# QR sign recursion of a rotation stage: Gram pivots and sign pivots of the same 32 columns in one loop, beside moved weight and constant work

## The chip, the cores and the metric

One core of a Trainium2 chip runs the whole program. Its engines work in parallel and meet at semaphores: TensorE (PE, with its weight loads as PEld), VectorE (DVE), ScalarE (ACT), GpSimd (POOL) and SyncE (SP), which issues the DMAs. The metric is the device time in microseconds of one execution.

## The reference, cut to what matters

Inputs are x (8 x 128 x 144) and a condition vector of 144 numbers for each of the 8 batch elements. Layer 0 rotates x inside the column space of a matrix P (144 x 64); three transformer layers with adaptive scale and shift, 16-head attention and a GELU MLP follow (24 visits of one batch element and layer).

```
def _rotation(cond, W, b):
    v = silu(cond) @ W.T + b                 # 2016 numbers for each batch element
    A = skew-symmetric 64 x 64 matrix from v
    return expm(A)                           # R, 64 x 64
# layer 0:  Q, _ = qr(P);  x = x + (x Q)(R - I) Q^T      (as the kernels compute it)
```

R comes from a polynomial and seven squarings. Q is not computed: with the Gram matrix G = P^T P and its Cholesky-like elimination, x Q follows from x P and the inverse factor. What remains of a Householder QR is the sign of each column, and those 64 signs come from a recursion over the top 64 x 64 part of P, one pivot after another.

## The kernel before

Everything here lies in one function, `program`, with one instruction list for each engine; the order in which the code is written is the order in which an engine executes. No scheduler changes it.

**The pivot work on DVE.** All of it is on 32-partition tiles, with three loops one after the other. Each `need(...)` waits for DVE's own counter, so an instruction that reads what the one before wrote waits for its completion.

- First loop (L1262 to L1301): 31 elimination steps of the leading 32 columns of G, in `lead`, with the inverse beside them. A step is four instructions: `spread` (a stream shuffle that copies row j to all 32 partitions, L1259), a reciprocal, a factor, an update of 64 columns. Some other work is put into steps 4, 6 and 24 (constants; the unpacking of the skew matrices, `LEAD_TAKES`).
- Second loop (L1320 to L1343): 32 steps on `work`, which holds the sign recursion of the leading half (columns 0 to 63) and the elimination of the trailing half of G (columns 64 on) side by side. A step is a 129-column spread, the sign fix of the pivot (L1326), a reciprocal of two numbers, two factors (L1330, L1332) and two updates (L1336, L1339).
- Third loop (L1368 to L1383): 31 steps of the sign recursion of the trailing half in `last`, five instructions each.

Between the loops, small products on TensorE (`lead_products`, `work_products`) form the Schur complement and turn factors; GpSimd takes one square root for each half (`root`, L405).

**What the other engines do meanwhile.** TensorE and ScalarE work through the list `pre` (`plan_rotation`): upper, skew, n2, mods, n4, gate 0, poly (1,0), gate 1, poly (1,1), gate 2, poly (0,0), xp, poly (0,1), two expm steps and the squarings. `lead_products` stands in TensorE's list behind n2 and `work_products` behind the squaring (4,1); each holds what is behind it until DVE's loop has ended. The last skew power, `raw`, the transposed `zT` (product of `linvT` and `xpT`) and DVE's scaling of `raw` by the signs (`rmi`, L1396) meet in the product that gives `yT`; from there it is a fixed path to the first visit.

**Weight remainders.** The last 17 rows of four weight matrices are used as three bf16 parts. For each layer ScalarE casts a part and makes a masked copy (`weight_part`, L575 and L577, into space of `gmod`), GpSimd subtracts it (`weight_left`, L411, 12 pieces of 102 x 268), and this is done twice.

**Constants.** GpSimd makes the scaled identities `eyes`, `irep` and `identb`, and TensorE's list waits for the last of them.

Of the kernel before, what the change touches and what calls it, by code (L numbers as in the profile page):

```python
# [26 lines left out]
BF16 = mybir.dt.bfloat16  # L27
# [7 lines left out]
D = 64  # L35
# [16 lines left out]
WSPLIT = NTAIL // 4  # L52
# [34 lines left out]
LEAD_TAKES = 24  # L87
FIRST_HALF_AFTER = ("n2", 0)
SECOND_HALF_AFTER = ("square", (4, 1))
# [7 lines left out]
def program(nc, t, out, spread_mods):  # L97
    ctx = ExitStack()
    with ctx:
# [41 lines left out]
        pick = sb("pick", [HALF, 2, HALF])  # L141
        nhalf_i = sb("nhalf_i", [HALF, D])
# [6 lines left out]
        lead = sb("lead", [HALF, 2 * D])  # L149
        work = sb("work", [HALF, D + 3 * HALF])  # L150
        ptop = sb("ptop", [HALF, D])
        g11 = sb("g11", [HALF, D])
        arow, brow, crow = sb("arow", [HALF, 2, 2 * D]), sb("brow", [HALF, 2, D + 3 * HALF]), sb("crow", [HALF, 2, HALF])
        arec, brec, crec = sb("arec", [HALF, HALF]), sb("brec", [HALF, HALF, 2]), sb("crec", [HALF, HALF])
        fac = sb("fac", [HALF, 2, 2])
        picked = sb("picked", [HALF, 2, HALF])
        dq, dr = sb("dq", [HALF, 1]), sb("dr", [HALF, 2])
        rs = sb("rs", [HALF, 2])
        scaled = sb("scaled", [HALF, D])
        m0T = sb("m0T", [HALF, HALF])  # L160
        wl = sb("wl", [HALF, HALF])
        zz = sb("zz", [D, HALF])
        last = sb("last", [HALF, HALF])
        sgn = sb("sgn", [HALF, 2])
# [13 lines left out]
        def halves(k):  # L178
# [16 lines left out]
        tprod = gmod[0:KS, 1:3, :, :].rearrange("p l b g -> p (l b g)")[:, 0:LAYERS * NTAIL].rearrange(  # L195
            "p (l n) -> p l n", l=LAYERS)
# [41 lines left out]
        ld = {n: sem("ld_" + n) for n in ("cond", "p", "skw", "x", "misc", "ada0", "ada1", "ada2",  # L238
                                          "blk0", "blk1", "blk2", "tail0", "tail1", "tail2", "tmask", "gmod0", "gmod1", "gmod2")}
        loads = {"cond": 3, "p": 4, "skw": 3, "x": 3, "misc": 3, "ada0": 3, "ada1": 2, "ada2": 2,  # L240
# [9 lines left out]
        lead_done, lead_turned, scaled_ready, m0T_ready = sem("lead_done"), sem("lead_turned"), sem("scaled_ready"), sem("m0T_ready")  # L250
        schur_full, top_full = sem("schur_full"), sem("top_full")
        dq_ready, rs_ready = sem("dq_ready"), sem("rs_ready")
        work_done, wl_ready, linv_turned = sem("work_done"), sem("wl_ready"), sem("linv_turned")
        wp_full, zz_ready, last_full, last_ready = sem("wp_full"), sem("zz_ready"), sem("last_full"), sem("last_ready")
# [6 lines left out]
        tail_cast, tail_left, tailw_ready = sem("tail_cast"), sem("tail_left"), sem("tailw_ready")  # L261
        act_step = sem("act_step")
# [38 lines left out]
        def _(sp):  # L301
# [8 lines left out]
            load(ptop[:], t["ptop"], "p")  # L310
            load(pT2[:], t["pT2"], "p")
# [4 lines left out]
            for l in range(LAYERS):  # L316
                load(tails[:, l, :], t[f"tail{l}"], f"tail{l}")
            for l in range(LAYERS):
# [21 lines left out]
            for l in range(LAYERS):  # L340
                if l == 1:
                    sp.wait_ge(tail_left, 2 * LAYERS)
# [22 lines left out]
        def _(pool):  # L365
# [16 lines left out]
            filled(lead[:, D:2 * D], 1.0).then_inc(early_consts, 1)  # L382
            pool.wait_ge(early_consts, 1)
            step(g.memset(half[:], 0.5))
            step(filled(work[:, D + 2 * HALF:D + 3 * HALF], 1.0))
            step(filled(ident[:], 1.0))
            step(g.memset(notj[:], -1.0))
            step(g.tensor_tensor(notj[:], notj[:], ident[0:HALF, 0:HALF], ALU.add))
# [1363 lines left out]
```

## Time and profile before

| | us |
|---|---|
| three runs | 436.83, 434.18, 437.65 |
| their median | 436.83 |
| the profiled execution | 434.67 |
| its span from first to last instruction | 432.8 |
| first pivot shuffle on DVE | 6.87 |
| second loop begins / third loop begins | 41.76 / 102.37 |
| product of `rmi` and `zT` begins | 137.38 |

The profile is of one execution; its rows give the time from the start of the span, the duration, engine, line, operation, output<-inputs and shapes. Line numbers are those of the kernel before. A duration is from start to completion, so two neighbours on one engine may overlap; the distance of their starts tells how soon the second could go. "PEclk 0.50" is the lower of TensorE's two clock levels (1.2 GHz), 1.00 the higher (2.4 GHz).

### The profile page before, as it was taken

What the parts mean: (1) busy time and instruction counts of PE and PEld (TensorE: products, weight loads), DVE (VectorE), ACT (ScalarE), POOL (GpSimd) and SP (SyncE); (2) the same over time, 40 slices, a digit from 0 to 9 for tenths busy, and PEclk for the clock granted to TensorE, in tenths of its full rate; (3) what the DMA queues carried; (4) which work ended last, traced back from release to release, by engine and by line L of the source; (5) the groups of instructions that cost most, each with busy time, mean ns of one, the idle gap of its engine ahead of it and who ended that gap; (6) DMA issues with size and microseconds to landing.
All of it is one profiled execution on the core that took longest, in us unless ns stands there. A gap on an engine that the chain in (4) does not pass through costs nothing.

```text
span 432.8 us, 10670 instructions
## 1 busy us (share of the span) xinstructions
PE 309.1 (71%) x3653; PEld 223.9 (52%) x3653; DVE 319.5 (74%) x1311; ACT 235.0 (54%) x494; POOL 154.2 (36%) x507
## 2 busy tenths in 40 slices
PE   1705987006003468889999999999999989898746
PEld 0704636005002234657777777777666666667534
DVE  4888999888886464877777877777989898877120
ACT  1420156002301225679787887978787878686721
POOL 7102508001600321253435353444555545442140
PEclk9999998556655555999999999999999999999978
DMA  5685000760000000000000000000000000000000
GB/s 167 198 251 172 0 0 5 195 207 1 0 1 0 2 0 2 2 2 2 5 2 2 2 3 3 2 2 3 2 2 2 3 2 2 2 16 2 15 15 14
DMA packets 10092, 14.10 MB, mean 33 GB/s; under 512 B 1674, under 2 KB 8558, under 8 KB 9912
## 3 DMA queue, kind: packets, MB, share of 16 engines
q1 hardware_dynamic: 10040, 13.43, 10.6%
q8 instruction: 30, 0.49, 0.5%
q14 instruction: 22, 0.18, 0.1%
HBM read 12.80 MB, written 0.62 MB: 31 GB/s over the span
## 4 chain that ended last, share of the span: by engine, by line
DVE 35%; PE 26%; issue 19%; POOL 10%; ACT 8%; SPq 1%; DMA 0%; POOLq 0%; ACTq 0%; DVEq 0%
PE ps L823 18%; DVE nmax L1498 5%; PE ps L1067 4%; DVE brow L1326 3%; DVE brow L1259 2%; ACT skw_r L707 2%; DVE lead L1275 2%; DVE fac L1330 2%; DVE work L1336 2%; PE ps L1124 2%; DVE arow L1259 2%; DVE work L1339 2%; ACT brief L668 2%; DVE fac L1272 2%; ACT L699 1%
## 5 line engine op out<-in xcount | busy, mean ns | idle before, releaser
L1498 DVE TENSOR_REDUCE nmax<-ps 128x4 f32<-128x512 f32 x96 | 62.6, 684 | 30.1 <-PE ps L823 30.0
L682 ACT ACTIVATE skw_t<-ps 128x512 f32<-128x512 f32 x96 | 53.4, 595 | 21.6 <-PE ps L823 21.4
L823 PE MATMUL ps<-skw_r 54*128 54x128 bf16 x768 | 48.4, 224 | 6.0 <-DVE nmax L1498 4.0
L823 PEld LDWEIGHTS ps<-skw_r 54*128 54x128 bf16 x768 | 30.1, 97 | 27.6 <-issue 18.9
L508 POOL TENSOR_TENSOR rstd<-vare,nhalf 128x1 f32<-128x1 f32 x24 | 13.2, 551 | 85.2 <-DVE vare L1416 68.5
L823 PE MATMUL ps<-mT_t,fc1w_t 128*128 128x256 f32 x120 | 39.8, 424 | 1.4 <-ACT mT_t L720 1.3
L823 PE MATMUL ps<-fc2w,skw_r 128*128 128x144 f32 (+1 forms) x240 | 34.2, 290 | 0.6 <-ACT skw_r L707 0.6
L675 ACT ACTIVATE skw_r<-ps 128x512 bf16<-128x512 bf16 x48 | 26.0, 594 | 12.5 <-PE ps L1067 12.1
L823 PEld LDWEIGHTS ps<-fc2w,skw_r 128*128 128x128 f32 (+1 forms) x240 | 30.8, 190 | 2.4 <-ACT skw_r L707 1.3
L1067 PE MATMUL ps<-identb,brief 128*128 128x128 bf16 x384 | 26.9, 226 | 4.9 <-DVE brief L1485 4.7
L699 ACT ACT_TABLE_LOAD x23 | 29.5, 1283 | 0.4
L823 PE MATMUL ps<-nmT,sel 64*128 64x128 bf16 x384 | 28.6, 222 | 0.0
L1067 PEld LDWEIGHTS ps<-identb,brief 128*128 128x128 bf16 x384 | 24.0, 102 | 7.1 <-issue 6.7
L823 PE MATMUL ps<-qkvw_t,hT_t 128*128 128x432 f32 x48 | 25.3, 612 | 0.8 <-ACT hT_u L728 0.8
L823 PEld LDWEIGHTS ps<-mT_t,fc1w_t 128*128 128x128 f32 x120 | 19.2, 201 | 8.9 <-issue 5.0
L494 POOL TENSOR_TENSOR tail<-ln,gmod 128x16 f32<-128x16 f32 x48 | 11.0, 229 | 35.1 <-DVE ln L1429 28.3
L823 PE MATMUL ps<-skw_t,brief 128*32 128x128 f32 x512 | 22.0, 288 | 1.1 <-ACT skw_t L682 1.1
L823 PE MATMUL ps<-skw_t,skw_r 64*64 64x128 f32 x16 | 2.0, 422 | 28.9 <-DVE skw_r L1396 28.9
L411 POOL TENSOR_TENSOR tails<-tails,gmod 102x268 f32<-102x268 f32 x24 | 17.1, 744 | 14.3 <-ACT gmod L577 14.3
L689 ACT ACTIVATE skw_t<-ps 128x512 f32<-128x512 f32 x24 | 14.0, 584 | 11.5 <-PE ps L823 11.1
L707 ACT ACTIVATE skw_r<-ps 128x512 f32<-128x512 f32 (+1 forms) x36 | 18.3, 509 | 3.5 <-PE ps L823 3.5
L668 ACT ACTIVATE brief<-ps 128x432 bf16<-128x432 f32 x32 | 17.7, 561 | 3.3 <-PE ps L823 3.3
(262 smaller groups left out, 813.6 us busy)
## 6 DMA issues: line engine op xcount, KB each, us to landing
gmod<-spread_mods SPq DMA_DIRECT2D x3, 1408.0 KB, 12.7
adaw_t<-in_ada SPq DMA_DIRECT2D x3, 432.0 KB
tails<-in_tail SPq DMA_DIRECT2D x3, 427.1 KB
skw_t<-in_skw SPq DMA_DIRECT2D x1, 1024.0 KB
fc1w_t<-in_fc SPq DMA_DIRECT2D x3, 320.0 KB
fc2w<-in_fc SPq DMA_DIRECT2D x3, 288.0 KB
qkvw_t<-in_qkv SPq DMA_DIRECT2D x3, 216.0 KB
x<-in_x SPq DMA_DIRECT2D x1, 576.0 KB, 6.3
```

Of the source, the lines that this page charges most:

```text
L411: i = g.tensor_tensor(w, w, tprod[:, l, c * WSPLIT:(c + 1) * WSPLIT], ALU.add)
L508: g.tensor_tensor(rstd[:, 0, h:h + 1], vare[:, 0, h:h + 1], nhalf[:, 0:1], ALU.pow).then_inc(rstd1, 1)
L668: a.activation(dst, src, ACT.Copy).then_inc(first_parts, 1)
L675: a.activation(qkT[1][v % 2][:, n:n + 4, :].rearrange("p k t -> p (k t)"), ps[:, 7, :].bitcast(BF16)[:, n * T:(n + 4) * T], ACT.Copy).then ...
L682: a.activation(prob[g].rearrange("p i t -> p (i t)"), ps[:, 2 + g % 2, :], ACT.Exp, scale=SCALE).then_inc(prob_ready, 1)
L689: a.activation(o_raw[v % 2].rearrange("p g t -> p (g t)"), ps[:, 4, :], ACT.Copy).then_inc(o_raw_ready, 1)
L699: a.activation(table_out[:], half[:], f).then_inc(table_used, 1)
L707: a.activation(hid[0:rows, 2 * r:2 * r + n, :, :].rearrange("p c h t -> p (c h t)"), ps[0:rows, FC1_BANKS[r], 0:n * 2 * T], f).then_inc(hi ...
L823: return pe.matmul(o, lhsT, rhs, start=start, stop=stop, skip_group_check=True)
L1067: i = pe.transpose(o[:, pair * T:(pair + 1) * T], parts[k][v % 2][:, 2 * pair:2 * pair + 2, :].rearrange("p h d -> p (h d)"), identb[:])
L1259: return did(d.stream_shuffle(out_, rows, [j] * HALF))
L1498: d.tensor_reduce(nmax[:, v % 2, first:first + 7:2], ps[:, 6 + g % 2, :].rearrange("p (i t) -> p i t", i=4), AX_X, ALU.max, negate=True).t ...
```

## The change

1. The signs are found another way. Per column the new kernel uses beta = sqrt(pivot of G) with the sign of the top entry, den = entry + beta, and updates the top rows with a numerator that uses the elimination factor `gfac` of the same column. So step j of the sign recursion needs step j of the elimination in the same half, and a square root for each column. These 64 roots are single-column powers on GpSimd (`root_of`), which read the pivot that the shuffle has written to a ring of four rows, `grow`.
2. There are two loops on DVE in place of three. In the first, sign step j of the leading half (`top[0]`, 64 columns shrinking to 33) and elimination step j+2 of the leading half alternate; in the second the same for the trailing half (`top[1]`, 32 columns shrinking to 1) with elimination step j+1.
3. Between them three block products on TensorE (`z_product` behind gate 0, `schur_products` behind poly (1,0), `turn_product` behind poly (1,1)) give the trailing Gram matrix and the trailing top part.
4. The product with `linvT` and its copy come at the end of the second loop (after elimination step 30 and sign step 30).
5. Weight remainders: TensorE computes tails - high - middle in PSUM by an identity product in fp32 and masked bf16 identity products (`left`, `rest`), in seven pieces of 512 columns behind "upper"; ScalarE casts each piece twice (`mid_part`, `low_part`). GpSimd's 24 subtractions and ScalarE's masked copies go.
6. ScalarE makes `eyes`, `irep` and `identb`. GpSimd's other small tasks are dealt out between its 64 roots; at roots 3, 46, 52 and 57 they carry waits for a load or for ScalarE. SP loads the top part of P in three pieces; the Gram product waits for two loads in place of four.

On DVE, in the steady part of the pivot work, a step of the second loop stood thus before (names as in the list above; f32 32-partition tiles):

```order
L1259 STREAM_SHUFFLE brow<-work 32x129 [waits dve_step]
L1326 SCALAR_TENSOR_TENSOR brow<-brow 32x1 [waits dve_step]
L1328 RECIPROCAL brec<-brow 32x2 [waits dve_step]
L1330 SCALAR_TENSOR_TENSOR fac<-work,brec,below 32x1 [waits dve_step]
L1332 SCALAR_TENSOR_TENSOR fac<-work,brec,notj 32x1
L1336 SCALAR_TENSOR_TENSOR work<-brow,fac,work 32x64 [waits dve_step]
L1339 SCALAR_TENSOR_TENSOR work<-brow,fac,work 32x55 [waits dve_step]
```

And thus a step of the changed kernel's first loop (trow, beta, den, tnum, drec, tfac, top are the sign recursion; grow, grec, gfac, lead the elimination):

```order
L1337 STREAM_SHUFFLE trow<-top 32x59 [waits dve_step]
L1371 SCALAR_TENSOR_TENSOR beta<-trow,root 32x1 [waits root_ready,dve_step]
L1359 SCALAR_TENSOR_TENSOR lead<-grow,gfac,lead 32x64 [waits dve_step]
L1377 TENSOR_SCALAR den<-trow,beta 32x1 [waits dve_step]
L1378 SCALAR_TENSOR_TENSOR tnum<-gfac,beta,top 32x1
L1381 RECIPROCAL drec<-den 32x1 [waits dve_step]
L1337 STREAM_SHUFFLE grow<-lead 32x65 [waits root_ready,dve_step]
L1385 SCALAR_TENSOR_TENSOR tfac<-tnum,drec,notj 32x1 [waits dve_step]
L1349 RECIPROCAL grec<-grow 32x1 [waits grow_ready]
L1392 SCALAR_TENSOR_TENSOR top<-trow,tfac,top 32x58 [waits dve_step]
L1353 SCALAR_TENSOR_TENSOR gfac<-lead,grec,below 32x1 [waits dve_step]
```

Seven instructions became eleven; between two that depend on each other there is now mostly one of the other recursion.

On TensorE, around the joint of the two loops, the changed list has the three block products between items of `pre`:

```order
L864 MATMUL ps<-kz,lead 32x32 [waits kz_ready,tailw_ready]
L864 MATMUL ps<-irep,eyes 128x256 [waits pre_read]
L864 MATMUL ps<-brief,eyes 128x256
L864 MATMUL ps<-base,zt 32x128 [waits z_ready,ld_base]
L864 MATMUL ps<-zt,base 32x32
L864 MATMUL ps<-adaw_t,s_t 8x352 [waits pre_read,ld_ada1]
L864 MATMUL ps<-adaw_u,s_bd 8x352
L864 MATMUL ps<-irep,eyes 128x256 [waits pre_read]
L864 MATMUL ps<-brief,eyes 128x256
L864 MATMUL ps<-vv,x1T 32x32 [waits vv_ready,x1T_ready]
```

DVE waits for the results of the products with `kz`, `zt` and `vv`; poly (1,0) stands before the second, gate 1 and poly (1,1) before the third.

The diff, cut to its core:

```diff
@@ GpSimd
+            def root_of(i):
+                p, j = i // HALF, i % HALF
+                pool.wait_ge(grow_ready, i + 1)
+                g.tensor_tensor(root[:, p, j:j + 1], grow[:, i % 4, 0:1], half[:], ALU.pow).then_inc(root_ready, 1)
...
-            root(0)
-            for l in range(LAYERS):
-                for c in range(4):
-                    weight_left(0, l, c)
...
+            for i in range(D):
+                root_of(i)
+                if i == 2:
+                    left_masks()
...
+                if 42 <= i < 42 + LAYERS:
+                    tail_mods(i - 42)
+                if i == 46:
+                    pool.wait_ge(pre_read, was_read("mods", 0))
+                if 46 <= i < 52:
+                    turned_mods((i - 46) // 2, i % 2)
...
+                if i == 57:
+                    pool.wait_ge(pre_read, pre_reads[-1])
...
@@ TensorE, behind "upper"
+            def left(c):
+                pe.wait_ge(high_ready, layers_of(c))
+                if c >= 3:
+                    pe.wait_ge(tailw_ready, c - 2)
+                at = chunk(c)
+                o = ps[0:KS, LEFT_BANKS[c % 3], 0:at.stop - at.start]
+                mm(o, ident[0:KS, 0:KS], tails_flat[:, at], True, False)
+                mm(o, dmask[:, 0, :], tailw_flat[:, at], False, False).then_inc(left_full, 1)
+            def rest(c):
+                pe.wait_ge(mid_ready, c + 1)
...
@@ VectorE, first loop of the changed kernel
+            for j in range(HALF):
+                e = j + 2
+                k_row = top_pivot(0, j)
+                k_beta = top_root(0, j, k_row)
+                if e < HALF - 1:
+                    gram_update(0, e, k_fac)
...
+                if j == HALF - 1:
+                    dve.wait_ge(schur_full, 1)
+                    loaded(dve, "base")
+                    k_late = did(d.tensor_tensor(late[:, 0:2 * D], base[1][:], ps[0:HALF, 7, 0:2 * D], ALU.subtract))
+                k_drec = top_denominator(0, j, k_beta)
+                if e < HALF - 1:
+                    gram_pivot(0, e + 1)
...
+                k_tfac = top_factor(0, j, k_drec)
+                if e < HALF - 1:
+                    k_rec = gram_reciprocal(0, e + 1)
...
+                top_update(0, j, k_tfac)
+                if e < HALF - 2:
+                    k_fac = gram_factor(0, e + 1, k_rec)
+                early_extras(j)
...
+            dve.wait_ge(top1_full, 1)
+            upd["t", 1] = did(d.tensor_tensor(top[1][:], late[:, HALF:D], ps[0:HALF, 6, 2 * D:2 * D + HALF], ALU.subtract))
```

## Rows read from the trace of the kernel before

**Rows 1.** Windows by stage: busy us (instructions) of each engine, granted clock, DMA share, GB/s.
```profile
0.00:41.80 41.80, 14.10 (x90) 12.22 (x90) 31.20 (x185) 9.75 (x13) 10.68 (x37) 1.00 0.69 203
41.80:100.20 58.40, 29.37 (x275) 19.06 (x275) 53.70 (x253) 14.56 (x30) 18.26 (x31) 0.78 0.27 76
100.20:136.90 36.70, 7.37 (x102) 5.66 (x102) 30.16 (x205) 7.15 (x10) 8.15 (x40) 0.59 0.00 0
136.90:173.40 36.50, 24.79 (x199) 15.64 (x200) 17.45 (x53) 12.27 (x30) 7.44 (x28) 0.50 0.00 1
```
**Rows 2.** Timeline, start of the pivot work: start us, us, engine, line, operation, shapes.
```profile
5.48 0.22 DVE L1251 TENSOR_TENSOR s_bd<-s_bd,own 119x56 f32<-119x56 f32 x1
...
6.61 0.21 DVE L1256 COPY lead<-ps 32x64 f32<-32x64 f32 x1 [0.92 <-PE ps L823]
```
**Rows 3.** DVE's timeline, two successive shuffles of the first loop.
```profile
30.60 0.21 DVE L1259 STREAM_SHUFFLE arow<-lead 32x65 f32<-32x65 f32 x1
...
31.59 0.21 DVE L1259 STREAM_SHUFFLE arow<-lead 32x65 f32<-32x65 f32 x1
```
**Rows 4.** DVE's timeline, one step of the second loop and the next shuffle.
```profile
50.67 0.28 DVE L1259 STREAM_SHUFFLE brow<-work 32x129 f32<-32x129 f32 x1
...
51.36 0.21 DVE L1330 SCALAR_TENSOR_TENSOR fac<-work,brec,below 32x1 f32<-32x1 f32 x1
51.49 0.20 DVE L1332 SCALAR_TENSOR_TENSOR fac<-work,brec,notj 32x1 f32<-32x1 f32 x1
51.62 0.27 DVE L1336 SCALAR_TENSOR_TENSOR work<-brow,fac,work 32x64 f32<-32x64 f32 x1
51.82 0.27 DVE L1339 SCALAR_TENSOR_TENSOR work<-brow,fac,work 32x62 f32<-32x62 f32 x1
...
52.12 0.28 DVE L1259 STREAM_SHUFFLE brow<-work 32x129 f32<-32x129 f32 x1
```
**Rows 5.** DVE's timeline, the third loop, from one sign fix on.
```profile
103.67 0.15 DVE L1374 SCALAR_TENSOR_TENSOR crow<-crow 32x1 f32<-32x1 f32 x1
103.86 0.15 DVE L1376 RECIPROCAL crec<-crow 32x1 f32<-32x1 f32 x1
104.04 0.21 DVE L1380 SCALAR_TENSOR_TENSOR fac<-last,crec,below 32x1 f32<-32x1 f32 x1
104.28 0.24 DVE L1382 SCALAR_TENSOR_TENSOR last<-crow,fac,last 32x30 f32<-32x30 f32 x1
```
**Rows 6.** Timeline, GpSimd's subtractions beside two instructions of DVE.
```profile
41.14 8.52 POOL L411 TENSOR_TENSOR tails<-tails,gmod 102x268 f32<-102x268 f32 x12
...
42.08 7.59 DVE L1326 SCALAR_TENSOR_TENSOR brow<-brow 32x1 f32<-32x1 f32 x1
...
68.91 0.78 DVE L1332 SCALAR_TENSOR_TENSOR fac<-work,brec,notj 32x1 f32<-32x1 f32 x1
```
**Rows 7.** Timeline, GpSimd's second root and DVE beside it.
```profile
100.78 0.57 POOL L405 TENSOR_TENSOR rs<-dr,half 32x1 f32<-32x1 f32 x1 [26.08 <-DVE dr L1350]
100.91 0.14 DVE L1353 TENSOR_SCALAR sgn<-dr 32x1 f32<-32x1 f32 x1
100.97 0.22 DVE L1355 COPY linvT<-ps 128x64 f32<-128x64 f32 x1
...
101.10 0.30 DVE L1358 SCALAR_TENSOR_TENSOR s<-sgn,rs 32x1 f32<-32x1 f32 x2
```
**Rows 8.** Timeline of TensorE and ScalarE: gates, zT, the first product behind the signs, a cast.
```profile
48.51 1.34 PE L823 MATMUL ps<-adaw_t,s_t 128*8 128x352 f32 x2
...
55.91 0.76 PE L823 MATMUL ps<-adaw_t,s_t 128*8 128x352 f32 x2
...
61.09 0.60 ACT L613 ACTIVATE skw_t<-ps 128x512 f32<-128x512 f32 x1 [1.63 <-PE ps L823]
...
107.20 1.08 PE L823 MATMUL ps<-skw_t,linvT 64*64 64x512 f32 x4 [0.48 <-ACT skw_r L608]
...
137.38 1.97 PE L823 MATMUL ps<-skw_t,skw_r 64*64 64x128 f32 x16 [28.86 <-DVE skw_r L1396]
```

More of the change, by code:

```diff
@@ L146, in program @@
         sel = sb("sel", [128, H, 128], BF16)
[L149 to L164, printed above, removed]
+        lead = sb("lead", [HALF, 4 * HALF])
+        late = sb("late", [HALF, 5 * HALF])
+        base = [sb(f"base{p}", [HALF, 4 * HALF]) for p in range(2)]
+        top = [sb("top0", [HALF, D]), sb("top1", [HALF, HALF])]
+        grow, trow = sb("grow", [HALF, 4, D + 1]), sb("trow", [HALF, 2, D])
+        grec, gfac = sb("grec", [HALF, 2, HALF]), sb("gfac", [HALF, 2, HALF])
+        root = sb("root", [HALF, 2, HALF])
+        beta, den, drec = sb("beta", [HALF, 2, HALF]), sb("den", [HALF, 2, HALF]), sb("drec", [HALF, 2, HALF])
+        tnum, tfac = sb("tnum", [HALF, 2]), sb("tfac", [HALF, 2])
+        pickg, pickd, picks = sb("pickg", [HALF, 2, HALF]), sb("pickd", [HALF, HALF]), sb("picks", [HALF, 2, HALF])
+        ginv, dinv = sb("ginv", [HALF, 2]), sb("dinv", [HALF, 1])
+        kz, zt = sb("kz", [HALF, HALF]), sb("zt", [HALF, HALF])
+        x1T, vv = sb("x1T", [HALF, HALF]), sb("vv", [HALF, HALF])
         s128 = sb("s128", [128, 1])
@@ new lines, in _, with gram_pivot @@
+            d.tensor_copy(lead[:, 0:D], ps[0:HALF, 7, 0:D]).then_inc(gram_read, 1)
+            dve.wait_ge(gram_read, 1)
+            elim = [lead[:], late[:, D:D + 3 * HALF]]
+            wide = [D, HALF]
+            upd = {("g", 0): 0, ("g", 1): 0, ("t", 0): 0, ("t", 1): 0}
+            def spread(rows, out_, j):
+                return d.stream_shuffle(out_, rows, [j] * HALF)
+            def gram_pivot(p, j):
+                i = HALF * p + j
+                need(upd["g", p])
+                if i >= 4:
+                    dve.wait_ge(root_ready, i - 3)
+                spread(elim[p][:, j:j + D + 1], grow[:, i % 4, :], j).then_inc(grow_ready, 1)
@@ new lines, in gram_update, with top_pivot @@
+            def gram_update(p, j, k_fac):
+                need(k_fac)
+                w = slice(j + 1, j + D + 1)
+                i = d.scalar_tensor_tensor(out=elim[p][:, w], in0=grow[:, (HALF * p + j) % 4, 1:D + 1],
+                                           scalar=gfac[:, p, j:j + 1], in1=elim[p][:, w], op0=ALU.mult, op1=ALU.add)
+                upd["g", p] = did(i)
+            def top_pivot(p, j):
+                need(upd["t", p])
+                w = slice(j, wide[p])
+                return did(spread(top[p][:, w], trow[:, j % 2, w], j))
@@ new lines, in top_root, with top_denominator @@
+            def top_root(p, j, k_row):
+                need(k_row)
+                dve.wait_ge(root_ready, HALF * p + j + 1)
+                return did(d.scalar_tensor_tensor(
+                    out=beta[:, p, j:j + 1].bitcast(U32), in0=trow[:, j % 2, j:j + 1].bitcast(U32), scalar=0x80000000,
+                    in1=root[:, p, j:j + 1].bitcast(U32), op0=ALU.bitwise_and, op1=ALU.bitwise_or))
+            def top_denominator(p, j, k_beta):
+                need(k_beta)
+                k_den = did(d.tensor_scalar(den[:, p, j:j + 1], trow[:, j % 2, j:j + 1], beta[:, p, j:j + 1], None, ALU.add))
+                did(d.scalar_tensor_tensor(out=tnum[:, j % 2:j % 2 + 1], in0=gfac[:, p, j:j + 1], scalar=beta[:, p, j:j + 1],
+                                           in1=top[p][:, j:j + 1], op0=ALU.mult, op1=ALU.subtract))
+                need(k_den)
+                return did(d.reciprocal(drec[:, p, j:j + 1], den[:, p, j:j + 1]))
```

490 lines of the change are left out of this document (264 added, 226 removed).

## The prediction

> **What bounds the kernel now.** I read the windows by stage first [rows 1]. Up to 136.9 us VectorE is busy 31.2 of 41.8, 53.7 of 58.4 and 30.2 of 36.7 us, while TensorE has 14.1, 29.4 and 7.4: the three pivot loops are one chain on DVE, and nothing of the transformer can start before it ends. The chain of waits says the same: in that stretch it runs along the lines of the pivot loops. So what the change is worth is read from where the product of `rmi` and `zT` starts, 137.38 us in the profiled execution [rows 8]; behind it nothing is edited.
>
> Then the timelines, for two different numbers of each instruction. The completion: each starts 0.03 to 0.04 us after the one it needs, as a factor at 104.04, 0.21 long, before an update at 104.28 [rows 5]. And the distance to an independent neighbour, which is shorter than a duration: the factors at 51.36 and 51.49 are 0.13 apart, an update of 64 columns lets the next go after 0.20 (51.62, 51.82) [rows 4], and a one-input `sgn` is followed after 0.06 by a copy [rows 7]. A step of the first loop takes 0.99 us [rows 3], of the second 52.12 - 50.67 = 1.45 [rows 4], both almost wholly waits for completion; that is the slack into which the change puts the other recursion.
>
> Third, what stalls DVE now. GpSimd's 12 subtractions run from 41.14 to 49.66, and the first sign fix beside them takes 7.59 us where such a fix has 0.15 [rows 6, 5]: 7.4 us lost. The second dozen stretches two-input instructions, as a factor of 0.78 for 0.20 [rows 6]: from the second loop's total, 100.24 - 41.76 = 58.5 us, less 32 x 1.45 = 46.4 less 7.4, about 4 more are lost there.
>
> **The change, step by step.** I lay the new pivot work out from its start.
>
> *Start.* The lead copy waits 0.92 us for the Gram product, now behind two early loads and not four; DVE's own work before it ends at 5.70 [rows 2]. Copy at 5.7, 0.9 earlier. Two elimination steps of 0.99 [rows 3] and a third without its update, 0.75: sign step 0 at 8.6.
>
> *A joint step*, 64 columns wide. Shuffle t at 0. beta at 0.25 (65 columns take 0.21 + 0.04 [rows 3]). The elimination's update at 0.32 (beta is of the kind of the one-input fix; 0.06 to 0.15, I take 0.07 [rows 7, 5]). den at 0.52 (0.20 behind the update [rows 4]), tnum at 0.65 (0.13). Reciprocal at 0.78, second shuffle at 0.87, tfac at 1.04, second reciprocal at 1.17, update of the top at 1.28 (tfac + 0.24 [rows 5]), gfac at 1.48 (0.20), next shuffle at 1.60. No row shows what may follow a shuffle or a reciprocal of a single column without a wait. From below they release like the one-input operation plus a column each (0.07 to 0.14), from above only on completion (0.25 and 0.18). I take 0.17 for the shuffle and 0.09 for the reciprocal, near the lower end, since all independent pairs on the page overlap. Bounds of a 64-wide step: 1.53 and 1.95. As the top narrows, its shuffle and its update shorten by about 1 ns for each column (0.27 for 64, 0.24 for 30 [rows 4, 5]), 2 ns together.
>
> *First loop.* 29 joint steps, 1.60 falling to 1.54, mean 1.57: 45.5. The put-in work (constants, unpacking; the steps with it are longer by about 0.3 + 0.8 + 1.1): 2.2. The last three signs have no elimination beside them but picks and copies: 5.0. End at 8.6 + 45.5 + 2.2 + 5.0 = 61.3, if nothing waits.
>
> *Joint.* z, Schur and turn products stand between gates and polynomials on TensorE. A gate product of 352 columns takes 1.34 us at 48.51 and 0.76 at 55.91 [rows 8], in the ratio of the two clock levels. At the slow level poly (1,0), two products of 256 columns at 1.34 x 256/352 = 1.0 each, holds the Schur product by about 2, gate 1 (2 x 1.34) and poly (1,1) hold the turn. Counting from kz: Schur result 1 us after DVE wants it, turn result about 2 us after. DVE's own work there (late subtraction, vv, x1T, two elimination steps): 2.6. At the fast level both waits shrink to some 0.5. I take the slow one: 1.0 + 2.6 + 2.0 = 5.6, so the second loop starts at 66.9.
>
> *Second loop.* 30 steps of mean 1.50 (32 columns down to 1): 45.0; sign scalings, one wait for the last elimination and its copy: 0.7; step 30: 1.3. Copy of linvT at 66.9 + 45.0 + 0.7 + 1.3 = 113.9.
>
> *End.* zT used to be made while DVE went through the third loop; now it comes last. At 107.20 it took 1.08 us with the clock granted; after some 20 us of idle TensorE I reckon twice that at most, take 1.9. With the copy of linvT (0.22), ScalarE's copy of 512 columns, 0.60 [rows 8], and hand-overs: 2.8. The signs on DVE need only about 1.4, so they are hidden. First product at 116.7.
>
> *Sum.* 137.4 - 116.7 = 20.7 us less.
>
> *At nothing:* the weight remainders. Seven identity products of about 1.1 us and 14 casts of at most 0.60 [rows 8] make 9 to 10 us on ScalarE between upper and skew, where TensorE and ScalarE have 28 and 32 us idle in the first window [rows 1]; `wup` is unpacked at sign step 10, at about 8.6 + 11 x 1.57 = 26, no later than the pieces end; it used to come in elimination step 24. If the cover were gone, `kz`'s product, which also waits for the last piece, would hold DVE; it is wanted only at about 8.6 + 30 x 1.57 = 56. The constants are hidden by the same idle 32 us of ScalarE: ten copies of at most 0.60. Roots: 0.57 each [rows 7] against a step of 1.5; even the longest small task between two of them (four dependent operations, some 1.4) fits in the two or three steps by which a pivot goes ahead. The spread of the gate values starts behind root 44, at about 80; 4.2 MB at the 200 GB/s of the first window [rows 1] take 21 us, first use at about 120.
>
> The profiled execution is 434.67 us for a span of 432.8, so the sum gives 434.7 - 20.7 = 414.0. The median of the three runs, 436.8, stands 2.2 above it, the lowest 0.5 below; I forecast **414**.
>
> **The shared port.** The root at 100.78 lasts until 101.35, and two two-input instructions of DVE at 101.10 beside it take 0.30 together, nothing longer than two alone [rows 7]; the subtractions of 268 columns stall DVE for long [rows 6]. So I price a root's hold on DVE at 0, with 0.1 us each (6 in all) as the upper end for a read at its start that no row isolates. The Trainium skill (SBUF — State Buffer, "SBUF: two separate sides") says that the port pair shared by VectorE and GpSimd is an exclusive lock, held for the whole instruction, and that the loser fully blocks. By that rule the sum would be that of the first rival; rows 6 agree with it, rows 7 do not.
>
> **Rivals.**
>
> 1. *The roots block DVE for their full time* (place: each joint step, at the update of the top, which follows the second shuffle that releases GpSimd). 0.57 from the shuffle's end leaves about 0.45 for the update to wait: 61 x 0.45 = 27 us, and if a second instruction waits too, 61 x 0.57 = 35. 414 + 27 = 441, up to 449, slower than before. It decides from 0.34 a step (20.7 / 61). For: 7.59 [rows 6]. Against: 101.10 [rows 7]. Chance 0.05.
> 2. *Shuffles and reciprocals do not overlap.* The step becomes 1.95 and 1.87: 59 x 0.36 = 21 us, 435, no gain. If the shuffle alone holds: 0.075 a step, 4.4 us, 418.5. For: no row behind a shuffle. Against: all others. First form 0.05; the second belongs to the forecast's range.
> 3. *A wait takes the gain's place:* late roots (GpSimd waits at root 57 for the last squaring; the list behind the turn product is less than the 29.4 us that TensorE is busy in the second window [rows 1], so 66 + 30 = 96, and root 57 falls at 66.9 + 23 x 1.5 = 101), or TensorE's slow clock at the joint. 5 to 12 us, 419 to 426. Chance 0.15.
> 4. *All goes well:* short intervals (4 us less), joint at the fast clock (2.5), the clock rising earlier in the first visits, which now run at the slow level for 36 us [rows 1] (up to 4): 403. Chance 0.15.
>
> The forecast itself has 0.60, with 408 to 421. Eight in ten: 402 to 427. One per cent, 4.4 us, is about what a measurement of this kernel can tell from no change. Faster by more (under 432.5): 0.90; within it 0.05 (rival 2 in full); slower 0.05 (rival 1).
>
> **What would show it.** Sign step 0 at 8.6 and unpacking at about 26; a joint step of 1.50 to 1.60 with tfac about 0.17 behind the second shuffle; no two-input DVE instruction longer beside a root than alone; DVE waits of about 1 and 2 us for PE at the joint; the second loop's start near 67, the first product with `rmi` near 117 and held by zT, not by the signs; no more 7 us instruction. It would be wrong if a step measures 1.9 or more, or if GpSimd's roots come after DVE asks for them.

## The result, and the profile after

| | before | changed |
|---|---|---|
| median of four runs, us | 435.66 | 411.92 |
| lowest and highest | 434.18 to 437.65 | 409.77 to 414.15 |
| profiled execution / its span | 434.67 / 432.8 | 414.15 / 412.3 |
| product of `rmi` and `zT` begins | 137.38 | 114.14 |
| from there to the end of the span | 295.4 | 298.2 |

The ratio of the medians is 0.946, interval 0.941 to 0.951: 23.7 us less. The forecast was 414. Medians here and below are of all executions of a kernel, ratios leave out three disturbed ones (1498.67 us with the products placed later, 438.89 us at a mean granted clock of 0.712 with the copy by ScalarE, 409.61 us with both moves).

The windows by stage (cut at the second loop's first sign shuffle and at the first product with `rmi`; columns as in [rows 1]):

```profile
0.00:65.06 65.06, 42.29 (x179) 26.10 (x180) 54.97 (x455) 17.68 (x42) 24.04 (x68) 0.78 0.45 132
65.06:114.10 49.04, 29.81 (x314) 18.20 (x312) 46.29 (x411) 10.31 (x24) 24.65 (x68) 0.60 0.32 91
114.10:150.60 36.50, 24.26 (x211) 16.20 (x212) 17.60 (x53) 12.78 (x31) 7.47 (x28) 0.64 0.00 0
```

DVE (the third busy time, behind PE's and PEld's) is still the chain: 55.0 of 65.1 and 46.3 of 49.0 us. Three stages [rows 1] have become two.

One joint step on DVE's timeline, which answers to [rows 4]:

```profile
51.08 0.18 DVE L1337 STREAM_SHUFFLE trow<-top 32x38 f32<-32x38 f32 x1
51.30 0.15 DVE L1371 SCALAR_TENSOR_TENSOR beta<-trow,root 32x1 uint32<-32x1 uint32 x1
51.37 0.27 DVE L1359 SCALAR_TENSOR_TENSOR lead<-grow,gfac,lead 32x64 f32<-32x64 f32 x1
51.57 0.20 DVE L1377 TENSOR_SCALAR den<-trow,beta 32x1 f32<-32x1 f32 x1
...
51.82 0.14 DVE L1381 RECIPROCAL drec<-den 32x1 f32<-32x1 f32 x1
51.90 0.22 DVE L1337 STREAM_SHUFFLE grow<-lead 32x65 f32<-32x65 f32 x1
52.04 0.20 DVE L1385 SCALAR_TENSOR_TENSOR tfac<-tnum,drec,notj 32x1 f32<-32x1 f32 x1
52.17 0.14 DVE L1349 RECIPROCAL grec<-grow 32x1 f32<-32x1 f32 x1
52.27 0.24 DVE L1392 SCALAR_TENSOR_TENSOR top<-trow,tfac,top 32x37 f32<-32x37 f32 x1
52.45 0.20 DVE L1353 SCALAR_TENSOR_TENSOR gfac<-lead,grec,below 32x1 f32<-32x1 f32 x1
52.59 0.18 DVE L1337 STREAM_SHUFFLE trow<-top 32x37 f32<-32x37 f32 x1
```

52.59 - 51.08 = 1.51. `tfac` is 0.14 behind the second shuffle, the update of `lead` 0.07 behind `beta`, though their durations are 0.22 and 0.15: independent instructions overlap, behind a shuffle too.

DVE's waits from 5 to 115 us, all of them:

```profile
DVE top L1489 <- PE ps L864: 1.9, 1, 1.9
DVE late L1447 <- PE ps L864: 1.0, 1, 1.0
DVE tfac L1385 <- issue: 0.2, 1, 0.2
```

And TensorE's timeline at the joint, where they come from:

```profile
57.06 0.28 PE L864 MATMUL ps<-kz,lead 32*32 32x32 f32 x2 [10.96 <-DVE kz L1465]
57.27 1.22 PE L864 MATMUL ps<-irep,eyes 128*128 128x256 f32 x2
58.29 1.06 PE L864 MATMUL ps<-brief,eyes 128*128 128x256 f32 x2
59.28 0.63 PE L864 MATMUL ps<-base,zt 32*32 32x128 f32 x2
...
59.95 1.34 PE L864 MATMUL ps<-adaw_t,s_t 128*8 128x352 f32 x2
...
63.50 1.06 PE L864 MATMUL ps<-brief,eyes 128*128 128x256 f32 x2
64.49 0.31 PE L864 MATMUL ps<-vv,x1T 32*32 32x32 f32 x2
```

Poly (1,0) stands between z and Schur, gate 1 and poly (1,1) between Schur and turn. But the first row also shows TensorE idle for 10.96 us ahead of `kz`.

The end of the pivot work (all engines), against [rows 8]:

```profile
108.69 0.27 DVE L1501 SCALAR_TENSOR_TENSOR late<-grow,gfac,late 32x64 f32<-32x64 f32 x1
...
109.25 0.41 PE L864 MATMUL ps<-ident,late 32*64 32x32 f32 x4
...
111.13 0.20 DVE L1530 COPY linvT<-ps 128x64 f32<-128x64 f32 x1
...
111.48 1.97 PE L864 MATMUL ps<-skw_t,linvT 64*64 64x512 f32 x4 [1.83 <-DVE linvT L1530]
...
112.31 0.48 DVE L1543 TENSOR_SCALAR skw_r<-skw_r,s 128x128 f32<-128x128 f32 x2
...
113.49 0.60 ACT L673 ACTIVATE skw_t<-ps 128x512 f32<-128x512 f32 x1 [15.22 <-PE ps L864]
...
114.14 1.97 PE L864 MATMUL ps<-skw_t,skw_r 64*64 64x128 f32 x16 [0.21 <-ACT skw_t L673]
```

The first product waits for ScalarE's copy of `zT`, not for `rmi`, ready at 112.8; and the copy of `linvT` starts 1.5 us behind its product because DVE has sign step 30 ahead of it.

GpSimd's roots, a group of the page (busy, mean ns):

```profile
L417 POOL TENSOR_TENSOR root<-grow,half 32x1 f32<-32x1 f32 x64 | 34.7, 542 | 56.6 <-DVE grow L1337 56.1
```

### The profile page after: what moved, and what is told of

It reads as the page before. It is cut to its first block, busy times and chain, and to the rows that moved or that the text cites. A ratio compares the mean times of both kernels' runs of the same rounds, so it can differ in the third digit from the quotient of the medians.

```text
span 412.3 us, 11130 instructions
## 1 busy us (share of the span) xinstructions
PE 331.8 (80%) x3680; PEld 233.1 (57%) x3680; DVE 305.6 (74%) x1532; ACT 231.6 (56%) x506; POOL 165.8 (40%) x536
## 4 chain that ended last, share of the span: by engine, by line
DVE 40%; PE 26%; issue 15%; ACT 9%; POOL 8%; DMA 0%; SPq 0%; POOLq 0%; ACTq 0%; DVEq 0%
PE ps L864 17%; DVE nmax L1645 5%; PE ps L1140 4%; DVE grow L1337 3%; DVE top L1392 3%; DVE trow L1337 3%; ACT skw_r L748 2%; DVE beta L1371 2%; ACT brief L709 2%; DVE den L1377 2%; PE ps L1197 2%; DVE tfac L1385 2%; DVE lead L1359 2%; ACT L740 2%; DVE st L1557 1%
## 5 line engine op out<-in xcount | busy, mean ns | idle before, releaser
L723 ACT ACTIVATE skw_t<-ps 128x512 f32<-128x512 f32 x96 | 53.4, 595 | 20.8 <-PE ps L864 20.5
L417 POOL TENSOR_TENSOR root<-grow,half 32x1 f32<-32x1 f32 x64 | 34.7, 542 | 56.6 <-DVE grow L1337 56.1
L1140 PE MATMUL ps<-identb,brief 128*128 128x128 bf16 x384 | 28.7, 234 | 5.2 <-DVE brief L1632 5.1
L1140 PEld LDWEIGHTS ps<-identb,brief 128*128 128x128 bf16 x384 | 25.6, 106 | 7.4 <-issue 7.0
L864 PE MATMUL ps<-qkvw_t,hT_t 128*128 128x432 f32 x48 | 26.3, 634 | 0.8 <-ACT hT_u L769 0.8
L864 PE MATMUL ps<-skw_t,brief 128*32 128x128 f32 x512 | 21.6, 284 | 1.1 <-ACT skw_t L723 1.1
L730 ACT ACTIVATE skw_t<-ps 128x512 f32<-128x512 f32 x24 | 14.0, 585 | 12.1 <-PE ps L864 11.7
L1639 DVE COPY skw_r<-ps 128x512 bf16<-128x512 bf16 x48 | 18.1, 418 | 2.3 <-PE ps L1140 2.3
```

The costliest lines, as they stand in the source:

```text
L417: g.tensor_tensor(root[:, p, j:j + 1], grow[:, i % 4, 0:1], half[:], ALU.pow).then_inc(root_ready, 1)
L723: a.activation(prob[g].rearrange("p i t -> p (i t)"), ps[:, 2 + g % 2, :], ACT.Exp, scale=SCALE).then_inc(prob_ready, 1)
L730: a.activation(o_raw[v % 2].rearrange("p g t -> p (g t)"), ps[:, 4, :], ACT.Copy).then_inc(o_raw_ready, 1)
L864: return pe.matmul(o, lhsT, rhs, start=start, stop=stop, skip_group_check=True)
L1140: i = pe.transpose(o[:, pair * T:(pair + 1) * T], parts[k][v % 2][:, 2 * pair:2 * pair + 2, :].rearrange("p h d -> p (h d)"), identb[:])
L1639: d.tensor_copy(qkT[0][v % 2][:, n:n + 4, :].rearrange("p k t -> p (k t)"), ps[:, 6, :].bitcast(BF16)[:, n * T:(n + 4) * T]).then_inc(qT_r ...
```

## The experiments

Each is told against the changed kernel's 411.92 where nothing else is said. The kernel before ran beside them, with medians of 434.7 to 437.1; the changed kernel did not, so a difference of 1 or 2 us in the medians decides nothing, and the start of the first product does. "First product" is the one of `rmi` and `zT`.

### What the old stalls were worth

```diff
             def weight_left(k, l, c):
...
-                i = g.tensor_tensor(w, w, tprod[:, l, c * WSPLIT:(c + 1) * WSPLIT], ALU.add)
                 if c == 3:
-                    i.then_inc(tail_left, 1)
+                    g.memset(spare[:, 3 * k + l:3 * k + l + 1], 0.0).then_inc(tail_left, 1)
```

> The kernel before with GpSimd's 24 subtractions left out (the remainder parts of the weights are then not formed); all else as before. Theory A (the stalls were worth what the sum says, 7.4 for the one long sign fix and about 4 in the second loop): 11.4 us less, 424.3, sign fix at its usual 0.15, first product with rmi at about 126. Then joining the recursions and the earlier start are worth the rest of the 23.7 us, about 12. Rival B (the stalled time is hidden by something else, so almost all of the change's gain is the joint loop): 2 us less or nothing, 434 to 436.

424.42 against 437.11, ratio 0.970 (0.964 to 0.976). The first product stands at 125.22, 12.2 us earlier, and the sign fix that took 7.59 [rows 6] is this:

```profile
42.31 0.15 DVE L1326 SCALAR_TENSOR_TENSOR brow<-brow 32x1 f32<-32x1 f32 x1
```

Theory A holds: about half of the change's gain (12.2 of 23.2 us at the first product) is the subtractions alone; the other 11.1 are the new pivot work and its earlier start (the copy into `lead` is at 5.66 for 6.61), which no run takes apart.

### The same instructions, not joined

```diff
                 k_beta = top_root(0, j, k_row)
                 if e < HALF - 1:
+                    k_drec = top_denominator(0, j, k_beta)
+                    k_tfac = top_factor(0, j, k_drec)
+                    top_update(0, j, k_tfac)
+                    need(upd["t", 0])
                     gram_update(0, e, k_fac)
+                    gram_pivot(0, e + 1)
+                    k_rec = gram_reciprocal(0, e + 1)
+                    if e < HALF - 2:
+                        k_fac = gram_factor(0, e + 1, k_rec)
+                        need(k_fac)
+                    early_extras(j)
+                    continue
```

(and the same in the second loop)

> The changed kernel with the same eleven instructions a step, but one recursion's after the other's: five of the signs with their completion waits, then the elimination's four, each waiting for the one before. Theory A (the joint step is short because one recursion runs in the other's waits): a step is 0.25 + 0.19 + 0.19 + 0.18 + 0.24 + 0.30 for the signs and 0.31 + 0.25 + 0.18 + 0.24 for the elimination = 2.33 where it has 1.48 and 1.43 now; 58 steps x 0.87 = 51 us more, 462. Rival B (the engine is bound by the number of instructions, so the order matters little): under 420.

459.25, ratio to before 1.052 (1.044 to 1.060); first product at 162.80. One step:

```profile
39.82 0.20 DVE L1337 STREAM_SHUFFLE trow<-top 32x52 f32<-32x52 f32 x1
...
41.21 0.27 DVE L1359 SCALAR_TENSOR_TENSOR lead<-grow,gfac,lead 32x64 f32<-32x64 f32 x1
...
42.21 0.20 DVE L1337 STREAM_SHUFFLE trow<-top 32x51 f32<-32x51 f32 x1
```

2.39 where the joint one has 1.54 (theory A had 2.33 and 462 in all), and the whole kernel is slower than before. Interleaved, eleven instructions cost about what the seven of the old second loop did (1.45 [rows 4]); the gain is that two such loops do the work of three.

### Roots on GpSimd: what holds DVE

```diff
+                g.tensor_tensor(spare[:, i:i + 1], half[:], half[:], ALU.pow)
```

behind each root.

> The changed kernel with a second power of one column behind each of GpSimd's 64 roots, into a tile that nobody reads. Theory A (a power does not hold DVE's port): GpSimd's 1.1 us a pivot still fit in a step of 1.43 to 1.48, DVE's two-input instructions keep 0.20 to 0.29; 412, within 2 us. Rival B (each power holds DVE for a part of its time, hidden in today's step lengths): 0.1 to 0.45 a step, 418 to 439, and DVE's two-input instructions get longer beside it. Rival C (GpSimd becomes late): waits of beta for root.

413.21. Steps and DVE's durations are those of the changed kernel but for three steps of the second loop where GpSimd has other tasks between its roots as well, and `beta` waits for it:

```profile
93.49 0.15 DVE L1373 SCALAR_TENSOR_TENSOR beta<-trow,root 32x1 uint32<-32x1 uint32 x1 [0.87 <-POOL root L418]
```

The first product comes 1.7 later (115.89). So A, with a little of C: a one-column power makes no DVE instruction beside it longer, and GpSimd's slack there is under one more root.

```diff
...
+                if 5 <= i < 29:
+                    w = gmod[0:KS, 0, 0, 0:268]
+                    step(g.tensor_tensor(w, w, w, ALU.add))
```

behind the root (a `memset` of those columns at root 3 is left out here).

> The changed kernel with one addition of 102 partitions x 268 columns (the size of the old subtractions) behind each of 24 of GpSimd's roots in the first loop, on memory that nobody reads. Theory A (a wide two-input operation holds DVE's two-input instructions for its own 0.7 us, a one-column power does not): some 0.5 to 0.7 us in each of 24 steps, 12 to 17 us more, 424 to 429, with single DVE instructions of 0.5 to 0.9 us in those steps. Rival B (only an unbroken row of such operations holds DVE, as the twelve in a row did): under 0.1 a step, 412 to 415.

433.56, 21.6 more than without (ratio to before 0.997): theory A in kind, but 0.94 a step and not 0.6. The timeline of GpSimd and DVE:

```profile
21.58 0.54 POOL L417 TENSOR_TENSOR root<-grow,half 32x1 f32<-32x1 f32 x1 [1.36 <-DVE grow L1342]
21.59 1.20 DVE L1397 SCALAR_TENSOR_TENSOR top<-trow,tfac,top 32x58 f32<-32x58 f32 x1
22.09 0.62 POOL L422 TENSOR_TENSOR gmod<-gmod 102x268 f32<-102x268 f32 x1
```

The update ends with the addition, at 22.7, yet had started half a microsecond before it. To tell whether the hold is a fixed one, the same additions were put ahead of the root:

```diff
                 pool.wait_ge(grow_ready, i + 1)
+                if 5 <= i < 29:
+                    w = gmod[0:KS, 0, 0, 0:268]
+                    step(g.tensor_tensor(w, w, w, ALU.add))
...
```

> The changed kernel with the same 24 additions of 102 x 268, but each ahead of its root and not behind it. With the addition behind, the update of the top took 1.20 for 0.25 and a step was 0.94 longer, more than the addition's own 0.62; the update had started with the root, half a microsecond ahead of the addition, and ended with the addition. Theory A (an addition holds DVE's two-input instruction from its own start to its end, and a root ahead of it only shifts that): with the addition first, the update that starts beside it takes some 0.6 more, a step is 0.6 longer, 412 + 24 x 0.6 = 426, unless beta then waits for the later root. Theory B (the hold is of a fixed 0.95, wherever the addition stands): 434 again.

420.76, ratio to before 0.966 (0.960 to 0.973).

```profile
21.48 0.63 POOL L419 TENSOR_TENSOR gmod<-gmod 102x268 f32<-102x268 f32 x1 [0.67 <-DVE grow L1342]
21.56 0.63 DVE L1397 SCALAR_TENSOR_TENSOR top<-trow,tfac,top 32x57 f32<-32x57 f32 x1
...
22.19 0.54 POOL L420 TENSOR_TENSOR root<-grow,half 32x1 f32<-32x1 f32 x1
```

The update again ends with the addition, now 0.63 long instead of 0.25: a step is 0.37 longer, 24 of them 8.9 us. I had expected the addition's whole 0.6 on top and forgot that DVE's own 0.25 runs inside it. B is out: with 268 columns the hold lasts to the addition's end in both places, and costs 0.37 a step ahead of a root and 0.94 behind it. Why it begins with the root there (GpSimd may take the operands of the next instruction while it computes a power) no run isolates.

The third of this kind varies size and operation:

```diff
...
+                for first, columns, op in ((5, 1, ALU.add), (21, 64, ALU.add), (34, 16, ALU.pow)):
+                    if first <= i < first + 8:
+                        w = gmod[0:KS, 0, 0, 0:columns]
+                        step(g.tensor_tensor(w, w, w, op))
```

> The changed kernel with one more GpSimd operation of 102 partitions behind a root, on memory that nobody reads: an addition of 1 column behind roots 5 to 12, an addition of 64 columns behind roots 21 to 28, a power of 16 columns behind roots 34 to 41. Theory A (what holds DVE is a streaming two-input addition, in proportion to its columns, and the fixed part of a power holds nothing): steps with 1 column as today (1.55), with 64 columns 0.1 to 0.3 longer, with the power of 16 columns as today. Theory B (any second operation right behind a root holds DVE from the root's start on, as the 268 columns did, where an update of 0.25 took 1.20): 0.6 a step longer in all three. Theory C (the column count alone counts, power or addition): 16 columns of power hold too.

```profile
16.85 0.54 POOL L417 TENSOR_TENSOR root<-grow,half 32x1 f32<-32x1 f32 x1 [1.65 <-DVE grow L1343]
16.86 0.29 DVE L1398 SCALAR_TENSOR_TENSOR top<-trow,tfac,top 32x59 f32<-32x59 f32 x1
...
43.33 0.54 POOL L417 TENSOR_TENSOR root<-grow,half 32x1 f32<-32x1 f32 x1 [0.86 <-DVE grow L1343]
43.34 0.38 DVE L1398 SCALAR_TENSOR_TENSOR top<-trow,tfac,top 32x43 f32<-32x43 f32 x1
...
43.85 0.28 POOL L423 TENSOR_TENSOR gmod<-gmod 102x64 f32<-102x64 f32 x1
...
72.92 2.90 POOL L423 TENSOR_TENSOR gmod<-gmod 102x16 f32<-102x16 f32 x1
73.04 0.15 DVE L1377 SCALAR_TENSOR_TENSOR beta<-trow,root 32x1 uint32<-32x1 uint32 x1 [2.02 <-POOL root L417]
...
74.03 0.23 DVE L1398 SCALAR_TENSOR_TENSOR top<-trow,tfac,top 32x27 f32<-32x27 f32 x1
```

Steps: 0.03 longer with one column, 0.13 with 64, 0.94 with 268 (from the run before the last). The power of 16 columns takes 2.90 us, and the DVE instructions beside it keep their 0.20 to 0.27; those steps are 2.0 longer (423.46 in all, one run), but only because the next root comes late. So theory A as to what holds, but not in proportion: 64 columns are 24% of 268 and cost 14% of its 0.94.

Two limits. The update beside the 64-column addition is longer by 0.13 and yet is over at 43.72, before that addition starts by the profile (43.85): its whole cost falls beside the root ahead of it, so "the hold lasts to the addition's end" is shown for 268 columns alone. And beside the roots ahead of the 16-column powers DVE was waiting for the root, with no two-input instruction under way; that a power takes nothing at that point is not shown, only that it holds nothing during its 2.90 us.

By the Trainium skill (SBUF — State Buffer, "SBUF: two separate sides"), whichever of VectorE (with two inputs in SBUF) and GpSimd starts first has their shared port pair for its whole instruction, and the other is blocked. The rows of the 268-column additions agree as to the end of the hold, but behind a root the update had started first (21.59 against 22.09) and was held all the same; the rows of the powers, up to 2.90 us long, do not agree.

### The two waits at the joint

```diff
-Z_AFTER = ("gate", 0)
-SCHUR_AFTER = ("poly", (1, 0))
+Z_AFTER = ("poly", (1, 1))
+SCHUR_AFTER = ("poly", (1, 1))
```

> The changed kernel with the products of kz and of the Schur complement behind poly (1,1) in TensorE's list, where the turn product already stands; TensorE is idle for 11 us before kz comes, which is more than poly (1,0), gate 1 and poly (1,1) take. Theory A (DVE's waits at the joint, 1.0 and 1.9, are those items in front of the products): both waits shrink to under 0.4, the second loop starts 2 to 2.5 earlier, 409.7. Rival B (the waits are the products themselves and their hand-overs): no change, 411.9. Rival C (the time comes back behind, by the clock of TensorE in the first visits): first product with rmi at 112, but 411 to 413 in all.

407.40, ratio to before 0.937 (0.932 to 0.942). The profiled execution was the one of 1498.67 us that is told of at the end, so the same kernel ran again:

> The kernel with the products of kz and of the Schur complement behind poly (1,1), once more, for a trace of an ordinary execution (the one before was of an execution of 1498 us in which every matmul took some three to five times its usual time). Its runs gave 407.4, 4.5 less than the changed kernel, where the two waits at the joint are 2.9 together. Theory A (both waits gone, the rest is the spread of runs): first product with rmi at 111.3 to 111.8, 2.4 to 2.9 earlier. Theory B (something else got shorter too, the squarings' chain or the stretch behind): first product by more than 3 earlier, or the stretch behind it shorter than 294.6.

408.98, ratio 0.940 (0.935 to 0.946). TensorE's timeline:

```profile
56.83 0.28 PE L864 MATMUL ps<-kz,lead 32*32 32x32 f32 x2 [4.64 <-DVE kz L1465]
58.03 0.60 PE L864 MATMUL ps<-base,zt 32*32 32x128 f32 x2 [0.93 <-DVE zt L1456]
...
60.37 0.31 PE L864 MATMUL ps<-vv,x1T 32*32 32x32 f32 x2 [1.63 <-DVE x1T L1481]
```

Now TensorE waits for DVE at each product and DVE for nothing. The second loop's first sign shuffle is at 61.76 for 65.06, the first product at 110.88, 3.3 earlier, of which 0.25 is already there at sign step 0 (8.22 for 8.47). By the number alone, more than 3, this is theory B's range, and theory A's 2.4 to 2.9 was too low. By the trace it is A: the whole of the 3.3 is there when the second loop starts, it is that 0.25 and the two waits (1.9 and 1.0), and nothing behind got shorter (49.1 us from there to the first product in both kernels, 295.1 from the first product to the end). Two series of this one kernel gave 407.40 and 408.98, so the rest of the first one's 4.5 is the spread of runs. Rival C did not come.

The slow clock's part shows in the run with small operations above, where the products stand as in the changed kernel: there the clock rose at the joint, the gate products took 1.23 and 0.75 us where both have 1.34 here, the two behind them 0.70 and 0.59 for 1.22 and 1.06, and DVE waited 1.0 and 0.2 us for 1.0 and 1.9.

### The copy of linvT

```diff
@@ VectorE, step HALF - 2
-                    dve.wait_ge(linv_turned, 1)
-                    d.tensor_copy(linvT[:], ps[:, 6, 0:D]).then_inc(linvT_ready, 1)
@@ ScalarE, ahead of its copy of zT
+            act.wait_ge(linv_turned, 1)
+            a.activation(linvT[:], ps[:, 6, 0:D], ACT.Copy).then_inc(linvT_ready, 1)
```

> The changed kernel with the copy of linvT made by ScalarE as soon as the late products are there, not by DVE behind sign step 30. Theory A (the end is held by linvT, zT and its copy, and the copy stands 1.4 behind its product because DVE has sign step 30 ahead of it): copy at 109.8, zT at about 110.2, first product with rmi 1.2 to 1.4 earlier, at 112.8, where the signs begin to bind; 410.6. Rival B (the signs bind already): no change. Rival C (given back by the clock behind): first product earlier, time the same.

409.29, ratio 0.941 (0.935 to 0.946), not clear of the changed kernel's 0.941 to 0.951 by itself. The trace decides: copy at 109.79, first product at 112.82, 1.3 earlier, as theory A had it; `rmi` is ready at about 112.8 too, so the signs bind from here on.

### TensorE kept busy before zT

```diff
+            pe.wait_ge(pre_read, pre_reads[-1])
+            for i in range(55, 62):
+                pe.wait_ge(root_ready, i)
+                for _ in range(3):
+                    mm(ps[:, 5, :], identb[0:KS, :], tailw_flat[:, 0:512])
             pe.wait_ge(late_done, 1)
```

> The changed kernel with 21 matmuls of 512 bf16 columns, read by nobody, on TensorE between the last squaring and the late products, three behind each of the roots 55 to 61, so that it is not idle for 13 us before zT. Theory A (zT at 1.97, the product with rmi at 1.97 and the first visits run at the lower clock because TensorE was idle before them): zT 1.1, product with rmi 1.1 to 1.2, together 2 to 3 less, and up to 3 more in the visits; 407 to 410. Rival B (the clock is lowered again behind the squarings whatever TensorE does): 412, or a little more when the visits get less of the higher clock.

412.01. The work was there and `zT` took as long as without it (granted clock 0.50 from 95 to 111 us):

```profile
97.02 10.05 PE L864 MATMUL ps<-tailw,identb 102*128 102x512 bf16 x21 [12.69 <-POOL root L417]
...
111.29 1.97 PE L864 MATMUL ps<-skw_t,linvT 64*64 64x512 f32 x4 [1.83 <-DVE linvT L1535]
```

Theory A is out for this work. Rival B ("whatever TensorE does") goes further than the run: its first row has TensorE idle for 12.69 us ahead of the added matmuls, and work set in right behind the squarings, with no idle time at all, is untested.

### The weight remainders left out

```diff
@@ left(c), rest(c), mid_part(c), low_part(c): 32 columns for up to 512
-                mm(o, ident[0:KS, 0:KS], tails_flat[:, at], True, False)
-                mm(o, dmask[:, 0, :], tailw_flat[:, at], False, False).then_inc(left_full, 1)
+                mm(o[:, 0:32], ident[0:KS, 0:KS], tails_flat[:, at.start:at.start + 32], True, False).then_inc(left_full, 1)
...
```

> The changed kernel with the seven pieces of the weight remainders cut to 32 columns each in TensorE's products and ScalarE's casts, with all semaphores kept (the remainder parts are then not formed). Theory A (that work lies wholly beside the first pivot loop): the same, 412 within 1; no DVE wait appears or goes. Rival B (it delays the skew chain and through it something DVE or the first product needs, or contends with DVE): 1 to 3 us less. Rival C (it keeps TensorE's clock up): more time than 412.

410.53, ratio 0.945 (0.938 to 0.951) where the changed kernel has 0.946. DVE's waits are the same three, 1.9, 1.0 and 0.2, and the first product, at 113.90, is no closer than the start of its pivot work is early (sign step 0 at 8.23 for 8.47). The median is 1.4 lower, which by itself would lie in rival B's range; by ratio and trace the remainders on TensorE and ScalarE cost nothing that can be seen. The higher mean granted clock of these executions (0.916 to 0.929 for 0.867 to 0.887) is no effect on the joint: the profile records 1.00 there, and yet the gate product takes the 1.34 us that it has at 0.50.

### Both moves

The edits of the products' places and of the copy of `linvT`, together.

> Both moves together: the products of kz and of the Schur complement behind poly (1,1), and the copy of linvT by ScalarE as soon as its product is there. Theory A (the two waits at the joint and the wait for DVE's copy are on one path, one behind the other): the gains add, first product with rmi at about 114.1 - 2.6 - 1.3 = 110.2, 411.9 - 3.9 = 408.0, or 405 if the single gains of 4.5 and 2.6 were whole. Rival B (one of them is hidden once the other is gone): no better than 407.4.

405.66 (402.78 to 409.61), ratio to before 0.932 (0.926 to 0.939), clear of the changed kernel's 0.941 to 0.951. First product at 109.51, 4.6 earlier:

```profile
106.49 0.22 ACT L673 ACTIVATE linvT<-ps 128x64 f32<-128x64 f32 x1 [21.71 <-PE ps L866]
...
109.51 0.90 PE L866 MATMUL ps<-skw_t,skw_r 64*64 64x128 f32 x5 [0.21 <-ACT skw_t L675]
```

(The view ends in the middle of the product, hence x5.) The gains add, as theory A had it: 3.3 + 1.3. This is the fastest version of the study, some 6 us below the changed kernel; by times alone it is not clear of the kernel with the products moved (0.932 to 0.942), but its first product is 1.4 earlier.

## Why the prediction was right

By its own terms, in us of the profiled execution:

| term | predicted | measured |
|---|---|---|
| sign step 0 | 8.6 | 8.47 |
| 29 joint steps with put-in work | 45.5 + 2.2 | 47.26 |
| last three signs and joint, to the second loop | 5.0 + 5.6 | 9.33 |
| second loop to the copy of `linvT` | 45.0 + 0.7 + 1.3 | 46.07 |
| copy to first product | 2.8 | 3.01 |
| first product | 116.7 | 114.14 |

**The step** was right, near the lower bound, as chosen: without put-in work it falls from 1.57 to 1.48 in the first loop (1.60 to 1.54 forecast) and from 1.50 to 1.43 in the second (mean 1.50 forecast). `tfac` follows the shuffle after 0.13 to 0.14, where I took 0.17. A few steps are 0.15 to 0.25 longer in every run, for instance with the update of `lead` 0.22 behind `beta` and not 0.07; that stays unexplained. The upper bound of 1.95 was worked out wrongly: with a shuffle released after 0.25 and a reciprocal after 0.18, the prediction's own chain ends at about 1.85, and rival 2 was worth some 15 us and not 21. Nothing hangs on it now.

**The joint** was placed right: waits of 1.0 and 1.9 for a forecast of 1.0 and 2.0, from poly (1,0) and from gate 1 with poly (1,1), at the slow clock; moving the products removed both. The three last signs and DVE's own work there took 6.4 where I had 5.0 + 2.6 = 7.6. "At the fast level both waits shrink to some 0.5" was half right: in the one run where the clock rose there, they were 1.0 and 0.2.

**The stalls** (7.4 + 4) measured 12.2. The prediction's own figures leave 58.5 - 46.4 - 7.4 = 4.7 for the second part, not 4, and 12.1 in all.

**At nothing:** the remainders were hidden (by the run without them), `wup` was unpacked at 26.72, and no wait at a root appears. The constants had no run of their own; TensorE's waits up to 115 us name none of them.

**The shared port**, rival 1, is refuted: doubling the power did not lengthen a two-input instruction. It was not an idle fear, though: 268-column additions behind 24 of the roots give back 21.6 us. **Rival 2** is refuted by the step. **Rival 3**: its slow clock at the joint was already in the forecast; its late roots did not come, although the last squaring ended at 96.1 and root 57 came at 100.9 (estimated 96 and 101). Of **rival 4** the short intervals came true; the recorded clock in the first 36.5 us of the visits was higher too (0.64 for 0.50), but the stretch from there to the end was not shorter for it.

**What went past the sum** is the time behind the first product. The profiled executions differ by 20.5 and the starts by 23.2. That 2.7 is no cost of the change: the same instructions there take 295.4 before and, in the twelve undisturbed profiles of the changed kernel and the experiments, 291.4 to 298.2, with differing stretches of the lower clock; the profiled execution of the changed kernel was the slowest of its four, at the lowest mean clock (0.867; the others 0.878 to 0.887). The medians, 23.7 apart, give back what the starts gained. So that the forecast of 414 meets the profiled 414.15 is luck: the first product came 2.6 earlier than forecast, and the stretch behind it, taken as unchanged, was 2.7 longer in that execution. Against the median of 411.9 it was 2 too high, mainly by the 2.6 at the first product; the mechanism and its terms hold.

## What to carry to other kernels

Where a chain of small dependent instructions leaves an engine waiting for its own completions, a second independent chain fits into the waits almost for free, even with more instructions: price the step from start-to-start distances, not from durations, and bound it by both. Look at what a neighbour on a shared port streams, not at how long it runs. Before placing a product that the bounding engine waits for, look at how long TensorE idles ahead of it: work that can be done in that idle time belongs in front.

## What the runs showed of the hardware

- GpSimd beside DVE's two-input update of 0.25 us: no DVE instruction is longer while a power of one column (0.54) or of 16 columns (2.90) runs; an addition of 1, 64 or 268 columns behind a root lengthens a step by 0.03, 0.13 and 0.94, and one of 268 ahead of the root by 0.37.
- 10 us of matmuls ahead of zT, begun after 12.7 us of idle TensorE, did not bring the higher clock: zT took 1.97 with them and without.
- The recorded granted clock can say 1.00 where matmuls have the durations of the lower level: the gate product takes 1.34 us at 59.71 us in the profile without remainders (recorded 1.00) and at 59.95 us in the changed kernel's (recorded 0.50). In the kernel before, too, the record is 1.00 from 46 to 58 us, while that product takes 1.34 at 48.51 and 0.76 at 55.91 [rows 8]. The durations decide.
- One execution of the kernel with the products placed later took 1498.67 us, with groups of matmuls at 2.2 to 4.3 times their mean and DVE's busy time as usual (309.8 for 305.6), at a recorded granted clock of 1.00. The same group of matmuls in the changed kernel's page and in that one:

```profile
L864 PE MATMUL ps<-fc2w,skw_r 128*128 128x144 f32 (+1 forms) x240 | 34.1, 290 | 0.6 <-ACT skw_r L748 0.6
```

```profile
L864 PE MATMUL ps<-fc2w,skw_r 128*128 128x144 f32 (+1 forms) x240 | 191.2, 1179 | 0.6 <-ACT skw_r L748 0.6
```

Nothing of it came back in the other nine runs of that kernel; the cause is open.
